# Feed-forward stage of a routed-expert kernel: eight written-out experts become one loop per engine

## The chip, the cores and the metric

One core of one Trainium2 chip runs the whole program. The metric is the device time of one execution in microseconds (us); the time before is 436.52 us, the median of 3 runs (436.09 to 436.82).

## The reference, cut to what matters

```python
x = x + conv_attention(_ln_c(x))           # 2 x 256 channels x 1024 places
t = _to_tokens(x); xt = _ln_t(t)           # 2048 tokens of 256
gate = softmax(xt @ Wg)                    # 8 experts
topv, topi = top_k(gate, 2)                # two experts for each token
for e in range(8):
    h = gelu(xt @ W1[e] + b1[e])           # 256 -> 1024
    ye = h @ W2[e] + b2[e]                 # 1024 -> 256
    out = out + ye * scores[:, e:e + 1]    # zero but for the two chosen
x = _from_tokens(t + out, x)
```

The change touches the loop over experts and nothing ahead of it.

## The kernel before

The first part (layer norm, attention, gates) takes about 170 us. It ends by sorting tokens by expert: `row_in` and `row_out` hold, for each tile, the rows to gather and to add to, and `bounds` holds for each expert e where its tiles end and two flags. `odd` says that its first tile is wide (`WIDE` = 3 blocks of 128 rows, not 2), `more` that it has further tiles of two blocks. With this input there are 17 tiles t; experts 0, 1, 3 and 7 have three each, expert 5 two, experts 2, 4 and 6 one, and the first tile of experts 0 and 5 is wide.

The feed-forward stage has no barrier: five engines each run their own program over the same tiles and meet through semaphores. Each program is a Python loop over the eight experts that writes the code out eight times: for each expert a wide first tile (`If(odd)`), a narrow first tile (`Else`) and a loop over further tiles (`If(more)`, `Fori`). In one tile:

- PE (TensorE) does `tile` (L1546): four `layer1` groups, then by turns `layer2(j-4)` and `layer1(j)` up to j = 7, then `turn_x` of the next tile (L1511, six transposes), then the last four `layer2`. Each product is three matmuls of high and low parts (`product3`, L1237 to 1239; L1538 to 1542). `layer1` may run four groups ahead (`RING`); `layer2(j)` waits for `h_split` of its own j (L1530).
- ScalarE (ACT) does two GELUs for each j (L802, L805). In an expert's first tile it also takes the high part of the next expert's weights, one eighth (`PIECE`) for each j (L815). Bias is a column of `b1t`.
- VectorE (DVE) takes `h_lo` (L1187) and in first tiles the low part of the weights (L1194). When PE has ended the tile it adds b2 (`y_sum`, L1203), waits for GpSimd's `y_free` and multiplies by the score (`y_out`, L1211), and goes to the next tile's `h_lo`.
- GpSimd (POOL) waits for `turn_x`, gathers the rows of the tile after next (L533, three indirect DMAs), sets `idx_out` (L571), lets DVE go (`y_free`, L574) and adds `y_out` to the output with indirect DMAs (L579).
- SP loads the raw weights of expert e once the split of expert e-1 is done (`load_expert`, L346).

So DVE's instructions stand in this order at the seam of two tiles, and PE's first `layer2` of the new tile waits for the last:

```python
    for i in range(width):
        ins = dve.tensor_scalar(y_out[:, i, :], ...)      # waits y_free
# ... end of the tile, branches ...
    dve.wait_ge(gelu_done, t * HJ + (j + 1 + RING))
    dve.tensor_tensor(h_lo[:, j, 0:w], ...).then_inc(h_split, 1)
```

`expert_bounds` (L340) loads the word of an expert from SBUF into a register (`value_load`, a TENSOR_LOAD) and takes it apart. ACT and DVE load all eight words ahead of the stage (L823, L1174); PE and POOL load one at each expert (L1573, L584 and L586).

## Time and profile before

| | |
|---|---|
| median of 3 runs | 436.52 us (436.09 to 436.82) |
| the profiled execution, its own time | 437.19 us |
| its span in the profile | 435.4 us |
| busy: PE / weight load / DVE / ACT / POOL | 373.3 / 334.5 / 267.0 / 248.1 / 185.5 us |
| instruction fetches: PE's queue (q8) / the other engines' (q14) | 28 packets, 0.46 MB / 27 packets, 0.22 MB |

The sum of a prediction is made against 437.19 us, of which 1.8 us lie outside the span; that execution stands 0.67 us above the median. A time at the head of a row is us from the span's start. "Idle" in brackets is the time in which that engine did nothing ahead of the row, and the arrow names what ended it; "issue" means that nothing in the profile did. A name with q (DVEq, PEldq) is the sequencer of that engine: the small instructions that set registers, load a word or branch, which the page doesn't count as busy.

### The profile page before, as it was taken

Reading aid. Unit: us, or ns where it says so; the run is one execution under the profiler, and the core shown is the slowest. Engines: PE = TensorE matmul, PEld = TensorE weight load, DVE = VectorE, ACT = ScalarE, POOL = GpSimd, SP = SyncE. Lnnn points to the kernel's source line nnn. Section 1 sums busy time; section 2 is a strip of 40 time slices with the busy share of each in tenths; the row PEclk is TensorE's granted clock in tenths of the full one; section 3 lists DMA queues with packets and bytes.
Section 4 is the critical chain, followed back from the end, with each engine's and each line's share of the span. In section 5 each row is a group of like instructions: output and inputs, shape, how many; then the busy total and the mean of one; then the engine's idle time right before and its main releaser. Section 6 shows DMA issues by size and latency. Waiting matters only on the chain.

```text
span 435.4 us, 8097 instructions
## 1 busy us (share of the span) xinstructions
PE 373.3 (86%) x2476; PEld 334.5 (77%) x2476; DVE 267.0 (61%) x684; ACT 248.1 (57%) x522; POOL 185.5 (43%) x279
## 2 busy tenths in 40 slices
PE   5889969989998657899999999799997999899960
PEld 4435557877787646899989998799987998799960
DVE  4668478796898995275447447584365754734430
ACT  1386557647516752385567467486575846655530
POOL 4610000003056565316656557535565265636553
PEclk9699999999996555799999999899999999989995
DMA  8710000000020754708324733648326434322332
GB/s 273 226 36 2 0 1 2 0 2 1 2 96 2 293 169 139 250 6 254 63 53 78 205 58 62 184 98 237 63 52 178 92 54 64 53 41 52 49 53 32
DMA packets 22983, 38.91 MB, mean 89 GB/s; under 512 B 2576, under 2 KB 17296, under 8 KB 22800
## 3 DMA queue, kind: packets, MB, share of 16 engines
q1 hardware_dynamic: 14896, 25.41, 17.3%
q0 software_dynamic: 8032, 12.82, 17.1%
q8 instruction: 28, 0.46, 0.4%
q14 instruction: 27, 0.22, 0.2%
HBM read 28.85 MB, written 9.37 MB: 88 GB/s over the span
## 4 chain that ended last, share of the span: by engine, by line
PE 35%; issue 8%; POOL 8%; DMA 4%; DVE 1%; POOLq 1%; DVEq 1%; ACT 0%; ACTq 0%
POOL xg L533 7%; PE banks L1538 6%; PE banks L1237 6%; PE banks L1238 5%; PE banks L1239 5%; PE banks L1540 5%; PE banks L1542 5%; PE banks L1515 3%; DMA xg<-xn_rows,idx_in 3%; DMA out_rows<-y_out,idx_out 1%; DVE h_lo L1187 1%; PE banks L1571 1%; DVE y_out L1211 1%; POOL out_rows L579 0%; POOL idx_out L571 0%
## 5 line engine op out<-in xcount | busy, mean ns | idle before, releaser
L802 ACT ACTIVATE h_raw<-banks,b1t 128x256 f32<-128x256 f32 (+1 forms) x136 | 67.2, 494 | 88.0 <-PE banks L1239 87.3
L1187 DVE TENSOR_TENSOR h_lo<-h_raw,h_hi 128x256 fp32r<-128x256 f32 (+1 forms) x136 | 58.8, 443 | 68.0 <-ACT h_hi L805 67.0
L1538 PE MATMUL banks<-w_hi,h_hi 128*128 128x256 f32 x288 | 83.8, 291 | 5.7 <-DVE h_lo L1187 5.6
L1237 PE MATMUL banks<-x_hi,w_hi 128*128 128x256 f32 (+1 forms) x272 | 81.0, 298 | 8.3 <-issue 8.3
L1540 PE MATMUL banks<-w_lo,h_hi 128*128 128x256 f32 x288 | 81.3, 282 | 0.0
L1542 PE MATMUL banks<-w_hi,h_lo 128*128 128x256 f32 x288 | 81.3, 282 | 0.0
L1238 PE MATMUL banks<-x_lo,w_hi 128*128 128x256 f32 (+1 forms) x272 | 79.9, 294 | 0.9 <-issue 0.9
L1239 PE MATMUL banks<-x_hi,w_lo 128*128 128x256 f32 (+1 forms) x272 | 79.9, 294 | 0.0
L579 POOL DMA_INDIRECT out_rows<-y_out,idx_out x36 | 61.4, 1705 | 33.7 <-DVE y_out L1211 27.9
L533 POOL DMA_INDIRECT xg<-xn_rows,idx_in x57 | 56.4, 990 | 28.0 <-POOL idx_in L528 15.4
L805 ACT ACTIVATE h_hi<-banks,b1t 128x256 fp32r<-128x256 f32 (+1 forms) x136 | 66.9, 492 | 0.0
L1538 PEld LDWEIGHTS banks<-w_hi,h_hi 128*128 128x128 f32 x288 | 54.9, 191 | 8.0 <-DVE h_lo L1187 8.0
L1237 PEld LDWEIGHTS banks<-x_hi,w_hi 128*128 128x128 f32 x272 | 53.5, 197 | 9.4 <-issue 9.3
L1540 PEld LDWEIGHTS banks<-w_lo,h_hi 128*128 128x128 f32 x288 | 55.0, 191 | 0.0
L1542 PEld LDWEIGHTS banks<-w_hi,h_lo 128*128 128x128 f32 x288 | 54.9, 191 | 0.0
L1239 PEld LDWEIGHTS banks<-x_hi,w_lo 128*128 128x128 f32 x272 | 53.4, 196 | 1.0 <-issue 1.0
L1238 PEld LDWEIGHTS banks<-x_lo,w_hi 128*128 128x128 f32 x272 | 53.6, 197 | 0.0
L470 POOL TENSOR_TENSOR rt<-rstd_i,rhv 128x4 f32<-128x4 f32 x12 | 2.5, 211 | 97.9 <-DVE rstd_i L1002 97.3
L1194 DVE TENSOR_TENSOR w_lo<-w_raw,w_hi 128x512 fp32r<-128x512 f32 x56 | 38.6, 689 | 0.7
L815 ACT ACTIVATE w_hi<-w_raw 128x512 fp32r<-128x512 f32 x56 | 36.4, 650 | 0.0
L692 ACT ACTIVATE pt_hi<-banks 128x512 fp32r<-128x512 f32 x32 | 17.5, 596 | 20.9 <-PE banks L1352 20.9
L1179 DVE TENSOR_TENSOR x_lo<-banks,x_hi 128x768 fp32r<-128x768 f32 x18 | 17.2, 958 | 13.1 <-ACT x_hi L792 12.8
(217 smaller groups left out, 686.4 us busy)
## 6 DMA issues: line engine op xcount, KB each, us to landing
w_raw<-in_w SPq DMA_DIRECT2D x16, 1024.0 KB, 7.8
xn_rows<-xn SPq DMA_DIRECT2D x2, 1056.0 KB, 4.7
x<-in_x_tok SPq DMA_DIRECT2D x4, 512.0 KB, 5.8
out_rows<-x SPq DMA_DIRECT2D x1, 2048.0 KB, 9.3
b2b<-in_b SPq DMA_DIRECT2D x1, 1024.0 KB, 4.4
xg<-xn_rows,idx_in POOLq DMA_INDIRECT x57
out_rows<-y_out,idx_out POOLq DMA_INDIRECT x36, 3.9
out_rows<-x POOLq DMA_DIRECT2D x1, 384.0 KB, 3.2
```

The lines of the kernel that those rows point to most:

```text
L533: pool.indirect_dma_start(xg[:, i, :], None, xs_d, bass.IndirectOffsetOnAxis(ap=idx_in[:, i:i + 1], axis=0)).then_inc(x_gathered, 16)
L579: pool.indirect_dma_start(out_d, bass.IndirectOffsetOnAxis(ap=idx_out[:, i:i + 1], axis=0), y_out[:, i, :], None, compute_op=ALU.add).then ...
L802: act.activation(h_raw[j % RING][:, 0:w], banks[:, j % RING, 0:w], ACT.Gelu, bias=bias)
L805: act.activation(h_hi[:, j, 0:w], banks[:, j % RING, 0:w], ACT.Gelu, bias=bias).then_inc(gelu_done, 1)
L1187: dve.tensor_tensor(h_lo[:, j, 0:w], h_raw[j % RING][:, 0:w], h_hi[:, j, 0:w].bitcast(F32), ALU.subtract).then_inc(h_split, 1)
L1194: dve.tensor_tensor(w_lo[(e + 1) % 2][:, c], w_raw[(e + 1) % 2][:, c], w_hi[(e + 1) % 2][:, c].bitcast(F32), ALU.subtract).then_inc(w_spli ...
L1237: pe.matmul(out, a_hi, b_hi, start=start, stop=False)
L1238: pe.matmul(out, a_hi, b_lo, start=False, stop=False)
L1239: return pe.matmul(out, a_lo, b_hi, start=False, stop=stop)
L1538: pe.matmul(out, h_hi[:, j, r], w_hi[e % 2][:, c], start=j == 0 and i < 2, stop=False, skip_group_check=width == WIDE)
L1540: pe.matmul(out, h_hi[:, j, r], w_lo[e % 2][:, c], start=False, stop=False, skip_group_check=width == WIDE)
L1542: ins = pe.matmul(out, h_lo[:, j, r], w_hi[e % 2][:, c], start=False, stop=j == HJ - 1, skip_group_check=width == WIDE)
```

## The change

PE runs a loop of four rounds over pairs of experts, with the two experts of a pair written out; ACT, DVE and POOL run a loop of eight rounds over one expert. What hung on a Python number now hangs on a register:

- each engine loads the expert's word of `bounds` inside the loop; the word now also holds the first tile;
- the two weight buffers become one tile with an index, fixed on PE (`odd` is 0 or 1 in the pair), chosen by a register on ACT and DVE; `w_loaded` is one semaphore that only grows, and SP waits for one load before it issues the next;
- ACT copies the expert's eight bias columns to `b1e` ahead of each expert and waits for that copy;
- DVE picks b2's and the score's columns by register;
- the last expert, too, splits "the next" weights (nobody reads that result), so one branch of the code is gone.

```diff
         def expert_bounds(eng, e):
-            word = eng.value_load(bounds[0:1, 0, e:e + 1], min_val=4, max_val=4 * TMAX + 3)
-            return word // 4, word % 4 // 2, word % 2
+            word = eng.value_load(bounds[0:1, 0, bass.ds(e, 1)], min_val=4, max_val=132 * TMAX + 3)
+            first = nc.s_assert_within(word // 128, 0, TMAX - 1, skip_runtime_bounds_check_because=why)
+            after = nc.s_assert_within(word % 128 // 4, 1, TMAX, skip_runtime_bounds_check_because=why)
+            return first, after, word % 4 // 2, word % 2
...
         def _(sp):
...
+                sp.wait_ge(w_loaded, 32 * e)
                 load_expert(sp, e)
+            sp.wait_ge(w_split, HJ * (E - 1))
+            sp.wait_ge(w_loaded, 32 * E)
+            sp.sem_inc(w_loaded, 32)
...
         def _(pool):
...
-            for e in range(E):
-                t1, odd, more = expert_bounds(pool, e)
-                odd1 = pool.value_load(bounds[0:1, 1, e:e + 1], min_val=0, max_val=E)
+            with pool.Fori(0, E) as e:
+                t0, t1, odd, more = expert_bounds(pool, e)
+                wides = pool.value_load(bounds[0:1, 1, bass.ds(e, 1)], min_val=0, max_val=17 * E)
+                odd0, odd1 = wides // 16, wides % 16
...
         def _(act):
...
-                    bias = b1t[:, e * HJ + j:e * HJ + j + 1]
+                    bias = b1e[:, j:j + 1]
...
-                    if split and e + 1 < E:
+                    if split:
                         if j == 0:
-                            act.wait_ge(w_loaded[(e + 1) % 2], 32 * ((e + 1) // 2 + 1))
+                            act.wait_ge(w_loaded, e * 32 + 64)
                             act.wait_ge(l2_done, t * HJ + HJ)
+                            act.sem_inc(splits_begun, 1)
...
-                        act.activation(w_hi[(e + 1) % 2][:, c], w_raw[(e + 1) % 2][:, c], ACT.Copy
-                                       ).then_inc(whi_done, 1)
+                        to = bass.ds((e + 1) % 2, 1)
+                        act.activation(w_hi[:, to, c].rearrange("p a c -> p (a c)"),
+                                       w_raw[:, to, c].rearrange("p a c -> p (a c)"), ACT.Copy).then_inc(whi_done, 1)
...
-            experts = [expert_bounds(act, e) for e in range(E)]
...
-            for e in range(E):
-                t1, odd, more = experts[e]
+            with nc.Fori(0, E, engines=[act.engine], head_slot={act.engine: 0}) as e:
+                t0, t1, odd, more = expert_bounds(act, e)
+                act.wait_ge(gelu_done, t0 * HJ + RING)
+                act.sem_inc(splits_begun, 1)
+                act.activation(b1e[:, :], b1t[:, bass.ds(e * HJ, HJ)], ACT.Copy).then_inc(b1_ready, 1)
+                act.wait_ge(b1_ready, e + 1)
...
         def _(dve):
...
-                    if split and e + 1 < E:
+                    if split:
...
-                        dve.wait_ge(whi_done, HJ * (e + 1) + j + 1)
+                        dve.wait_ge(whi_done, HJ * e + (HJ + j + 1))
...
-                                            b2b[:, e * C:(e + 1) * C], ALU.add)
+                                            b2b[:, bass.ds(e * C, C)], ALU.add)
...
-                    ins = dve.tensor_scalar(y_out[:, i, :], y_sum[:, i, :], score[:, i, e:e + 1], None, ALU.mult)
+                    ins = dve.tensor_scalar(y_out[:, i, :], y_sum[:, i, :], score[:, i, bass.ds(e, 1)], None, ALU.mult)
...
-            for e in range(E):
-                t1, odd, more = experts[e]
+            with nc.Fori(0, E, engines=[dve.engine], head_slot={dve.engine: 0}) as e:
+                t0, t1, odd, more = expert_bounds(dve, e)
...
         def _(pe):
...
-            for e in range(E):
-                t1, odd, more = expert_bounds(pe, e)
-                with pe.If(odd):
-                    tile(t0, e, WIDE, True)
...
+            with pe.Fori(0, E // 2) as pair:
+                for n in range(2):
+                    e = pair * 2 + n
+                    t0, t1, odd, more = expert_bounds(pe, e)
+                    with pe.If(odd):
+                        tile(t0, e, n, WIDE, True)
...
```

The static program of PE shrinks from 3,239 rows (runs of equal instructions) to 1,063, DVE's from 1,063 to 417, ACT's from 938 to 251 and POOL's from 497 to 163.

DVE, the seam between an expert's last tile and the next expert's first. An ISA row is a register operation. Before:

```order
L1211 TENSOR_SCALAR y_out<-y_sum,score 128x256 [waits y_taken,scores_moved,y_free]
L1211 TENSOR_SCALAR y_out<-y_sum,score 128x256
L1228 ISA
L1228 COMPARE_AND_BRANCH
L1227 UNCONDITIONAL_BRANCH
L1223 ISA
L1223 COMPARE_AND_BRANCH
L1185 ISA
L1186 REGISTER_ALU [waits gelu_done]
L1187 TENSOR_TENSOR h_lo<-h_raw,h_hi 128x384 [waits l2_done]
```

And now, the end of the round and behind it the head of the next (to which the branch of L1235 goes back):

```order
L1226 REGISTER_ALU [waits y_taken,scores_moved,y_free]
L1226 TENSOR_SCALAR y_out<-y_sum,score 128x256
L1226 ISA
L1226 TENSOR_SCALAR y_out<-y_sum,score 128x256
L1242 ISA
L1242 COMPARE_AND_BRANCH
L1241 UNCONDITIONAL_BRANCH
L1235 REGISTER_ALU
L1235 COMPARE_AND_BRANCH
```

```order
L1235 ISA
L344 TENSOR_LOAD bounds
L344 ISA x2
L1237 ISA
L1237 COMPARE_AND_BRANCH
L1197 ISA
L1198 REGISTER_ALU [waits gelu_done]
```

Between the wait for `y_free` and the first `h_lo` there now stand also a register operation ahead of each `y_out`, the count and branch of the outer loop, and the load of the expert's word, which stood ahead of the whole stage before.

ACT, the same seam, before (its load stood ahead of the stage) and now:

```order
L792 ACTIVATE x_hi<-banks 128x768 [waits xg_turned]
L829 ISA [waits bias_loaded]
L829 COMPARE_AND_BRANCH
L802 ACTIVATE h_raw<-banks,b1t 128x384 [waits h_split,l1_ready]
```

```order
L835 ISA
L344 TENSOR_LOAD bounds
L344 ISA x2
L837 ISA
L839 ISA [waits gelu_done]
L839 ACTIVATE b1e<-b1t 128x8
L840 REGISTER_ALU
L841 ISA [waits b1_ready]
L841 COMPARE_AND_BRANCH
```

ACT gains the load, the bias copy and a wait for its own copy, ahead of each expert's first GELU.

## Rows read from the trace of the kernel before

**Rows 1.** The page, busy time: engine, us, share of the span, instructions.
```profile
PE 373.3 (86%) x2476; PEld 334.5 (77%) x2476; DVE 267.0 (61%) x684; ACT 248.1 (57%) x522; POOL 185.5 (43%) x279
```

**Rows 2.** Waits, 180 to 436 us: engine and line, releaser: us, times, longest.
```profile
PE banks L1237 <- issue: 8.3, 5, 2.5
...
PE banks L1538 <- DVE h_lo L1187: 5.6, 10, 1.0
```

**Rows 3.** Timeline of PE, `turn_x` of nine tiles: start us, us.
```profile
259.24 0.82 PE L1515 MATMUL banks<-ident,xg 128*128 128x128 f32 x6
272.69 0.82 PE L1515 MATMUL banks<-ident,xg 128*128 128x128 f32 x6
289.08 0.82 PE L1515 MATMUL banks<-ident,xg 128*128 128x128 f32 x6
...
314.78 0.49 PE L1515 MATMUL banks<-ident,xg 128*128 128x128 f32 x3
328.23 0.82 PE L1515 MATMUL banks<-ident,xg 128*128 128x128 f32 x6
347.01 0.82 PE L1515 MATMUL banks<-ident,xg 128*128 128x128 f32 x6
361.63 0.82 PE L1515 MATMUL banks<-ident,xg 128*128 128x128 f32 x6
375.26 0.82 PE L1515 MATMUL banks<-ident,xg 128*128 128x128 f32 x6
391.41 0.82 PE L1515 MATMUL banks<-ident,xg 128*128 128x128 f32 x6
```

**Rows 4.** Timeline of PE, matmuls behind a pause: the pause stands in brackets.
```profile
213.85 0.38 PE L1538 MATMUL banks<-w_hi,h_hi 128*128 128x256 f32 x1 [0.44 <-DVE h_lo L1187]
...
266.83 0.39 PE L1538 MATMUL banks<-w_hi,h_hi 128*128 128x256 f32 x1 [1.01 <-DVE h_lo L1187]
278.85 0.56 PE L1237 MATMUL banks<-x_hi,w_hi 128*128 128x256 f32 x1 [2.48 <-issue]
...
334.29 0.43 PE L1237 MATMUL banks<-x_hi,w_hi 128*128 128x384 f32 x1 [2.38 <-issue]
353.84 0.28 PE L1238 MATMUL banks<-x_lo,w_hi 128*128 128x256 f32 x1 [0.87 <-issue]
...
381.18 0.49 PE L1237 MATMUL banks<-x_hi,w_hi 128*128 128x256 f32 x1 [2.24 <-issue]
```

**Rows 5.** Timeline of DVE at the seam of experts 1 and 2.
```profile
265.20 0.62 DVE L1211 TENSOR_SCALAR y_out<-y_sum,score 128x256 f32<-128x256 f32 x2 [1.39 <-POOLq L574]
...
266.35 0.43 DVE L1187 TENSOR_TENSOR h_lo<-h_raw,h_hi 128x256 fp32r<-128x256 f32 x1 [0.54 <-ACT h_hi L805]
```

**Rows 6.** Sequencers, by line: count, ns min/median/max, first and last start us.
```profile
L1574 PEldq COMPARE_BRANCH  x10: 73/348/2818, 178.7 to 378.3; - x10
...
L343 DVEq TENSOR_LOAD <-bounds x8: 297/304/558, 170.0 to 174.6; - x8
...
L1223 DVEq COMPARE_BRANCH  x1: 72/72/72, 265.6 to 265.6; - x1
...
L1185 DVEq FUSED_REGOPS  x1: 106/106/106, 266.1 to 266.1; - x1
L1185 DVEq ALU_OP  x1: 40/40/40, 266.4 to 266.4; - x1
...
L1228 DVEq FUSED_REGOPS  x2: 63/79/95, 212.8 to 213.2; - x2
L1228 DVEq COMPARE_BRANCH  x1: 69/69/69, 213.0 to 213.0; - x1
```

**Rows 7.** Windows: us, length, busy (x) of five engines, granted clock, DMA share, GB/s.
```profile
279.00:282.00 3.00, 3.00 (x15) 3.00 (x16) 0.79 (x4) 1.49 (x4) 1.64 (x1) 0.50 0.93 346
...
332.00:335.00 3.00, 0.71 (x4) 0.72 (x5) 1.37 (x4) 0.00 (x0) 1.80 (x3) 1.00 0.94 272
...
382.00:385.00 3.00, 3.00 (x17) 3.00 (x17) 0.42 (x1) 1.68 (x4) 1.99 (x2) 0.55 0.25 41
```

More of the change, by code:

```diff
@@ L119, in metaformer_kernel @@
         s_w = ctx.enter_context(ExitStack())
-        w_hi = [sb(f"w_hi{i}", [P, WCOLS], F32R, s_w) for i in range(2)]
-        w_lo = [sb(f"w_lo{i}", [P, WCOLS], F32R, s_w) for i in range(2)]
+        w_hi = sb("w_hi", [P, 2, WCOLS], F32R, s_w)
+        w_lo = sb("w_lo", [P, 2, WCOLS], F32R, s_w)
         with ExitStack() as s:
@@ L226, in metaformer_kernel @@
         bias_loaded = sem("bias_loaded")
-        w_loaded = [sem(f"w_loaded{i}") for i in range(2)]
+        b1_ready = sem("b1_ready")
+        w_loaded = sem("w_loaded")
+        splits_begun = sem("splits_begun")
         consts_made = sem("consts_made")
@@ L593, in _ @@
                         tile(t, e, t * 2 + odd1, 2)
-                t0 = t1
-                odd0 = odd1
-            pool.wait_ge(y_added, t1 * 32 + odd1 * 16 + 16)
-            pool.wait_ge(x_gathered, (t1 + 2) * (16 * WIDE))
+            last = expert_bounds(pool, E - 1)[1]
+            wide = pool.value_load(bounds[0:1, 1, E - 1:E], min_val=0, max_val=17 * E) % 16
+            pool.wait_ge(y_added, last * 32 + wide * 16 + 16)
+            pool.wait_ge(x_gathered, (last + 2) * (16 * WIDE))
         @block.scalar
@@ L814, in tile @@
                             x_high(t + 1)
-                        act.activation(w_hi[(e + 1) % 2][:, c], w_raw[(e + 1) % 2][:, c], ACT.Copy
-                                       ).then_inc(whi_done, 1)
-                if not (split and e + 1 < E):
+                        to = bass.ds((e + 1) % 2, 1)
+                        act.activation(w_hi[:, to, c].rearrange("p a c -> p (a c)"),
+                                       w_raw[:, to, c].rearrange("p a c -> p (a c)"), ACT.Copy).then_inc(whi_done, 1)
+                if not split:
                     x_high(t + 1)
@@ L1173, in _ @@
             dve.wait_ge(bounds_ready, 2)
-            experts = [expert_bounds(dve, e) for e in range(E)]
             def x_low(n):
@@ L1517, in turn_x, with layer1 @@
                 ins.then_inc(xg_turned, 1)
-            def layer1(t, e, j, width):
+            def layer1(t, odd, j, width):
                 pe.wait_ge(gelu_done, t * HJ + (j + 1))
@@ L1537, in layer2, with tile @@
                     out = banks[:, 4 + i % 2, i // 2 * C:(i // 2 + 1) * C]
-                    pe.matmul(out, h_hi[:, j, r], w_hi[e % 2][:, c], start=j == 0 and i < 2, stop=False,
+                    pe.matmul(out, h_hi[:, j, r], w_hi[:, odd, c], start=j == 0 and i < 2, stop=False,
                               skip_group_check=width == WIDE)
-                    pe.matmul(out, h_hi[:, j, r], w_lo[e % 2][:, c], start=False, stop=False,
+                    pe.matmul(out, h_hi[:, j, r], w_lo[:, odd, c], start=False, stop=False,
                               skip_group_check=width == WIDE)
-                    ins = pe.matmul(out, h_lo[:, j, r], w_hi[e % 2][:, c], start=False, stop=j == HJ - 1,
+                    ins = pe.matmul(out, h_lo[:, j, r], w_hi[:, odd, c], start=False, stop=j == HJ - 1,
                                     skip_group_check=width == WIDE)
                 ins.then_inc(l2_done, 1)
-            def tile(t, e, width, new):
+            def tile(t, e, odd, width, new):
                 pe.wait_ge(x_split, t + 1)
@@ L1567, in _ @@
             pe.wait_ge(bounds_ready, 2)
-            t0 = 0
             turn_x(0)
```

63 lines of the change are left out of this document (32 added, 31 removed).

## Prediction

> **What bounds the kernel now.** I read the page first: PE is busy 86% of the span [rows 1], so time is gained only where PE stands still. The waits from 180 us on, the feed-forward stage, say where it does: 8.3 us in five pauses that nothing in the profile ends, and 5.6 us in ten waits of `layer2` for `h_lo` [rows 2]. The timeline of PE gives the places [rows 4]. Three long pauses, 2.48, 2.38 and 2.24 us, stand ahead of the first tiles of experts 3, 5 and 7, each right behind a single-tile expert (2, 4, 6), whose loop code is jumped over. One of 0.87 us is in expert 5's second tile. The reader is to see what these pauses are: a compare-and-branch on PE's sequencer, usually 348 ns, took up to 2818 ns [rows 6]. I take that for the wait for code: it happens where code is skipped, and never in a loop's second pass.
>
> The other pauses have another owner. At the seam of experts 1 and 2 I follow the order of the code: `turn_x` at 259.24 [rows 3], then POOL's gathers, then `y_out` at 265.20 (5.96 us behind the turn), then `h_lo` at 266.35 [rows 5], then PE's first `layer2` at 266.83 after 1.01 us of waiting [rows 4]. So from one turn to the first `layer2` it is 7.59 us, set by POOL and DVE and not by PE, which was there at 6.58. DVE's own part is 1.15 us from `y_out` to `h_lo`, and the multiply is only 0.62 of it: the rest is branches and registers. A tile inside a loop waits on the same chain, for 0.44 us [rows 4]. **Any instruction added between `y_out` and `h_lo` is paid in full, at every tile.**
>
> I measure from turn to turn [rows 3]. Seams with no code pause take 13.45 us (expert 2: 259.24 to 272.69; expert 4: 314.78 to 328.23); expert 1, whose rows aren't shown, I take as equal. Expert 3 takes 16.39, expert 7 16.15, expert 6 13.63, the wide tile of expert 5 18.78.
>
> **What goes.** With loops, code is fetched once and the long pauses go. But PE then runs into the DVE chain, which it missed before because it was late. A seam can't be shorter than the 13.45 us of an undisturbed one, so of the pauses of 2.48 and 2.24 us experts 3 and 7 give back 2.94 and 2.70 (part of it is the clock, below), expert 6 0.18. Expert 5 gives back at most its 2.38, its second tile at most 0.87.
>
> **What comes, on DVE, part by part.**
> - In every tile: a register operation (40 ns) takes over the wait for `y_free`, and a fused one (106 ns) stands between the `y_out`s [rows 6]. With some 50 ns between instructions I take 0.2 us.
> - At each seam, the outer loop's count and branch: 40 ns and 72 ns, and the landing. A taken branch in the inner loop lands within 0.13 us (213.07 to 213.2), one over the wide tile's code needs 0.43 (265.67 to 266.1) [rows 6]. From both sides: 0.3 to 0.6 us with the gaps. The way back to the head is longer than either, so I take a value near the upper one.
> - At each seam, a fused operation for the address: 0.15 us.
> - At each seam, the load of the word. One takes 304 ns, but what stands behind it has to be done too: eight groups of load, unpacking and assertion began between 170.0 and 174.6 us, 0.66 us apart [rows 6]. They cost nothing there, since DVE waited for the first gather; in the loop nothing covers them.
>
> Sum for a seam: 0.2 + 0.3 to 0.6 + 0.15 + 0.66 = 1.3 to 1.6; I take 1.5 us. The Trainium skill (Advanced Engine Details and Errata, Control Flow Timing) gives about 108 ns for a compare-and-branch; by it the seam would be 1.2 us and the total below some 2 us less. The trace shows 72 ns for the instruction and up to 0.5 us until the next one, and I go by the trace.
>
> **What comes elsewhere.** PE: one load group and, in every second seam, the way back of the pair loop, some 0.1 to 0.6 us later at the first `layer1`. It waits for `h_lo` 1.01 + 1.5 us later on, which covers this. ACT: load group, bias copy, a wait for it, some 2.5 us in all by DVE's prices; ACT is free from the end of its `x_hi` until the next tile's first group, about as long, and `h_lo` of j = 0 now comes 1.5 us later than it did, so a late GELU is covered. POOL has two loads as before. SP's new wait is for a load that ended tens of us before. The last expert's split costs ACT and DVE eight pieces each, as in every other expert, and PE nothing but what the other seams show. The first `bounds` load of DVE falls between `x_lo(0)` and the first GELU; nothing.
>
> **Sum.** Experts 1, 2 and 4: 3 x 1.5 = +4.5. Expert 6: 13.45 + 1.5 against 13.63 = +1.3. Expert 3: 14.95 against 16.39 = -1.4. Expert 7: 14.95 against 16.15 = -1.2. Expert 5: `layer1` of a wide tile is half as long again (24 matmuls of 384 columns, not 256, at 2.4 GHz: 1.3 us more), so PE is there at 6.6 + 1.3 = 7.9 and `h_lo` at 7.6 + 1.5 = 9.1: the pause of 2.38 becomes one of 1.2, -1.2. Its second tile: -0.8. The other eight loop tiles at 0.2, less one behind a wide tile that has room: +1.4. The last `y_out`: +0.2. Together **+2.8 us**, and this holds already: about 9 us of pauses go and about 12 come.
>
> **The clock.** After the pause of 2.48 us the granted clock was 0.50 from 279 to 282, after the one of 2.24 it was 0.55 from 382 to 385; after the one of 2.38 it stayed at 1.00 [rows 7]. So a pause of this size halves the clock (2.4 to 1.2 GHz) sometimes, for some 3 us, and costs half of that, 1.5 us. The six narrow seams will now have pauses of 2.0 to 2.5 us at the first `layer2`, where three stood before. Nothing covers the loss there. Between no fall and six (0 to +9 us) I take one or two, **+2.2 us**, near what two falls in three pauses say for the seams with the longest pauses.
>
> In all +5.0: the profiled execution would be at 442.2, and since it stands 0.67 us above the median, the forecast is **441.5 us**.
>
> **Rivals.**
> - *The seam is cheap, and the kernel faster.* If the branch back lands at once and the load runs beside the `y_out`s, a seam costs 0.9 instead of 1.5: 7 x 0.6 = 4.2 less, with no fall of the clock 1.4 below before, 435.1 us. It decides below about 1.1 us a seam. For it: the multiply's 0.62 us could cover something. Against it: in the row of before `h_lo` comes 0.53 us after the `y_out`s have ended, so the sequencer was already the later one, and every addition stands behind it. Chance 0.10.
> - *The clock doesn't fall.* Then 436.5 + 2.8 = 439.3. For it: the pause of 2.38 us left the clock alone, and PE's late start splits the pause in two. Chance 0.22. The reverse, a fall at nearly every seam: 436.5 + 2.8 + 9 = 448. Chance 0.07.
> - *The code isn't kept.* Each way back could fetch its code anew. DVE's seven at 2.2 to 2.5 us (the pauses of rows 4) are 15 to 17 more, 455 us or over. Against it: an inner loop's second pass never shows such a pause. But these loops are far shorter. Chance 0.06. The Trainium skill (Runtime: NRT & Kernel Launch, Instruction fetch mechanics) speaks for this rival: it tells of a window of two pages with no reuse, out of which a taken branch stalls. No run here shows yet what a long loop does. If only PE fetches again, the DVE chain hides most of it and the forecast stands.
> - *The change does nothing:* the pauses stay as they are and the additions are covered, within 0.9 us of before. Chance 0.05.
>
> **How the numbers follow.** The forecast (seams longer, one to three falls, 439.5 to 445) has 0.50. A measurement of this kernel can tell about 0.2%, 0.9 us, from no change. Faster takes the first rival, 0.10; the same 0.07, from the last one and the edge of the first; slower 0.83. The range leaves out the cheap seam below and the many falls and new fetches above: 437 to 446.5.
>
> **What would show it.** No pause over 1 us "<- issue" on PE behind single-tile experts; at each narrow seam `layer2` waiting 2.0 to 2.5 us for `h_lo`; from `y_out` to `h_lo` some 2.6 us instead of 1.15; TENSOR_LOAD rows of DVE spread over the stage, eight in number; turn to turn about 14.9 us at seams; a granted clock of 0.5 behind some. Instruction fetches of PE's queue far below 28. Wrong would be: waits for `h_lo` at seams near 1 us, or fetches at every round.

## The result, and the profile after

| | before | changed |
|---|---|---|
| median, runs | 436.67 us, 4 | 448.65 us, 4 (445.98 to 449.0) |
| ratio | 1 | 1.0261 (1.0219 to 1.0303) |
| profiled execution, its span | 437.19, 435.4 us | 448.8, 447.1 us |
| fetches, PE's queue / the others' | 28 / 27 packets | 11 / 12 packets |

Slower by 2.6%, 12 us. The sign was forecast; the size (441.5, range up to 446.5) was not. The spans differ by 11.7 us, and the question is where these lie.

The page of the changed kernel, busy time (against [rows 1]), fetch queues, and its waits from 180 us on (against [rows 2]):

```profile
PE 375.7 (84%) x2476; PEld 335.9 (75%) x2477; DVE 272.7 (61%) x694; ACT 255.2 (57%) x539; POOL 183.2 (41%) x280
...
q8 instruction: 11, 0.18, 0.2%
q14 instruction: 12, 0.10, 0.1%
```

```profile
PE banks L1551 <- DVE h_lo L1199: 11.8, 11, 2.8
...
ACT b1e L839 <- issue: 9.5, 8, 6.3
...
PE banks L1551 <- issue: 8.2, 5, 2.0
...
PE banks L1251 <- issue: 3.1, 1, 3.1
```

Two things to see. PE's waits for `h_lo` have doubled, from 5.6 to 11.8 us, and the 8.2 us that nothing ends stand at the same matmul, L1551, the first `layer2` of a tile. It is the same chain: at expert 2, `h_lo` ends at 277.14 us and PE starts at 277.20. And two single waits are new: ACT 6.3 us ahead of its first bias copy, PE 3.1 us ahead of a `layer1` matmul.

From turn to turn, as in [rows 3] (timeline of PE):

```profile
196.62 0.82 PE L1528 MATMUL banks<-ident,xg 128*128 128x128 f32 x6
211.55 0.82 PE L1528 MATMUL banks<-ident,xg 128*128 128x128 f32 x6
...
241.54 0.82 PE L1528 MATMUL banks<-ident,xg 128*128 128x128 f32 x6
...
268.52 0.82 PE L1528 MATMUL banks<-ident,xg 128*128 128x128 f32 x6
283.05 0.82 PE L1528 MATMUL banks<-ident,xg 128*128 128x128 f32 x6
299.10 0.82 PE L1528 MATMUL banks<-ident,xg 128*128 128x128 f32 x6
...
325.38 0.82 PE L1528 MATMUL banks<-ident,xg 128*128 128x128 f32 x6
339.94 0.82 PE L1528 MATMUL banks<-ident,xg 128*128 128x128 f32 x6
357.21 0.82 PE L1528 MATMUL banks<-ident,xg 128*128 128x128 f32 x6
371.89 0.82 PE L1528 MATMUL banks<-ident,xg 128*128 128x128 f32 x6
386.40 0.82 PE L1528 MATMUL banks<-ident,xg 128*128 128x128 f32 x6
402.43 0.82 PE L1528 MATMUL banks<-ident,xg 128*128 128x128 f32 x6
```

Subtracting neighbours, and the same for the other kernels of this study (us; "stage's first turn" runs from the first `turn_x` of all, at 176 to 179 us, to the one in expert 0's first tile):

| interval that ends with the turn of | before | changed | word_ahead | dve_written | pe_loop_only | pe_loop_slot | all_cures_200 |
|---|---|---|---|---|---|---|---|
| expert 0, first tile | 16.68 | 19.74 | 18.46 | 20.19 | 15.67 | 15.66 | 16.65 |
| expert 0, second tile | 13.60 | 14.93 | 14.94 | 13.74 | 13.66 | 13.72 | 14.50 |
| expert 1, first | 13.49 | 16.86 | 17.08 | 18.11 | 17.44 | 13.62 | 13.92 |
| expert 2 | 13.45 | 14.53 | 13.90 | 13.56 | 13.57 | 13.57 | 13.91 |
| expert 3, first | 16.39 | 16.05 | 14.18 | 13.61 | 13.85 | 13.85 | 14.27 |
| expert 3, third (a loop tile) | 12.80 | 13.12 | 13.15 | 12.96 | 12.88 | 12.88 | 13.25 |
| expert 4 | 13.45 | 14.56 | 13.89 | 13.53 | 13.54 | 13.55 | 13.91 |
| expert 5, first (wide) | 18.78 | 17.27 | 16.86 | 16.36 | 16.23 | 16.15 | 16.94 |
| expert 6 | 13.63 | 14.51 | 13.81 | 13.50 | 13.50 | 13.51 | 13.92 |
| expert 7, first | 16.15 | 16.03 | 13.89 | 13.67 | 13.80 | 13.79 | 15.76 |

The first interval also hangs on the clock. From 177 to 180 us it was granted 0.52 in before and 0.50 in the changed kernel, from 178.2 to 181.2 us 1.00 in pe_loop_only and pe_loop_slot; their first interval, 1.0 us below that of before, is probably shorter for this and not for the loop. The 20.19 and 18.11 us of dve_written each have a fall of the clock in them.

**Two thirds of the loss lie in the first round.** From the stage's first turn (176.57 and 176.88) to that of expert 1 (233.19 and 241.54) the changed kernel takes 8.0 us more. From there to the last turn, thirteen tiles, it takes 187.44 us against 184.22, 3.2 more. The other 0.4 lie outside.

*The entry.* Timeline of ACT, the start of the stage, and of PE behind it:

```profile
178.50 0.81 ACT L801 ACTIVATE x_hi<-banks 128x768 fp32r<-128x768 f32 x1 [7.92 <-PE banks L1528]
185.63 0.21 ACT L839 ACTIVATE b1e<-b1t 128x8 f32 x1 [6.32 <-issue]
186.24 0.58 ACT L811 ACTIVATE h_raw<-banks,b1e 128x384 f32<-128x384 f32 x1 [0.41 <-ACT b1e L839]
```

```profile
188.05 0.39 PE L1551 MATMUL banks<-w_hi,h_hi 128*128 128x256 f32 x1 [2.83 <-DVE h_lo L1199]
```

ACT's bias copy starts 6.32 us behind its last work, and nothing in the profile ends that time; packets of the fetch queue q14 begin at 182.8, 183.9 and 185.6 us inside it. PE stands 2.83 us. I had written that ACT's late GELU is covered.

*Expert 1.* One matmul of `layer1` runs, and then:

```profile
228.29 0.38 PE L1250 MATMUL banks<-x_hi,w_hi 128*128 128x256 f32 x1
231.79 0.37 PE L1251 MATMUL banks<-x_lo,w_hi 128*128 128x256 f32 x1 [3.12 <-issue]
231.96 0.41 PE L1252 MATMUL banks<-x_hi,w_lo 128*128 128x256 f32 x1
```

One packet of q8 begins at 229.4 and takes 1.0 us, inside the 3.12 us. The matmuls behind it take 0.41 us, not 0.28: the clock fell, as after the long pauses of before.

*A seam, to compare with [rows 5].* Timeline of DVE at the seam of experts 1 and 2:

```profile
274.58 0.62 DVE L1226 TENSOR_SCALAR y_out<-y_sum,score 128x256 f32<-128x256 f32 x2 [1.39 <-issue]
276.72 0.42 DVE L1199 TENSOR_TENSOR h_lo<-h_raw,h_hi 128x256 fp32r<-128x256 f32 x1 [1.52 <-ACT h_hi L814]
```

From `y_out` to `h_lo` it is 2.14 us, where it was 1.15; I had said 2.6. The seams of experts 2 and 4 grew by 1.08 and 1.11 us, where I had said 1.5. The sequencer's rows for the load, the way back and PE's way back (count, ns min/median/max):

```profile
L344 DVEq TENSOR_LOAD <-bounds x8: 302/313/568, 180.1 to 393.4; - x8
L344 DVEq FUSED_REGOPS  x8: 190/197/210, 180.7 to 393.7; - x8
```

```profile
L1235 DVEq COMPARE_BRANCH  x9: 56/59/72, 179.4 to 435.5; - x9
L1235 DVEq FUSED_REGOPS  x8: 63/63/69, 180.0 to 393.3; - x8
```

```profile
L1584 PEldq COMPARE_BRANCH  x4: 83/212/216, 270.5 to 431.0; - x4
```

From the end of the branch back at this seam (275.14) to the next instruction (275.36) it is 0.22 us, at the others 0.22 to 0.25, and no way back shows a pause of a microsecond: **the code of the loops stays.** The last packet of PE's fetch queue begins at 250.3 us, and the three rounds behind it run without one; the last of the other engines' queue begins at 208.4.

The clock, windows as in [rows 7]:

```profile
231.00:234.00 3.00, 2.21 (x11) 2.21 (x11) 0.34 (x2) 0.95 (x3) 1.63 (x1) 0.54 0.22 45
291.00:294.00 3.00, 2.24 (x14) 2.25 (x15) 2.72 (x6) 2.87 (x7) 2.69 (x3) 0.78 1.03 313
294.00:297.00 3.00, 3.00 (x19) 3.00 (x19) 2.23 (x5) 1.93 (x5) 1.01 (x3) 0.65 0.93 187
334.00:337.00 3.00, 2.92 (x24) 2.93 (x25) 3.00 (x8) 2.94 (x7) 2.67 (x3) 1.00 0.37 44
395.00:398.00 3.00, 2.90 (x13) 2.90 (x14) 3.00 (x8) 2.21 (x6) 2.69 (x3) 0.51 0.39 44
```

It fell at experts 1, 3 and 7, and stayed at experts 2, 4 and 6. So the seams of experts 3 and 7 still take 16 us, some 14.5 for the chain and 1.5 for the clock, though PE's code pause is gone there.

### The profile page after: what moved, and what is told of

It reads as the page before. It is cut to its first block, busy times and chain, and to the rows that moved or that the text cites. A ratio compares the mean times of both kernels' runs of the same rounds, so it can differ in the third digit from the quotient of the medians.

```text
span 447.1 us, 8582 instructions
## 1 busy us (share of the span) xinstructions
PE 375.7 (84%) x2476; PEld 335.9 (75%) x2477; DVE 272.7 (61%) x694; ACT 255.2 (57%) x539; POOL 183.2 (41%) x280
## 4 chain that ended last, share of the span: by engine, by line
PE 39%; issue 9%; POOL 4%; DMA 3%; DVE 3%; DVEq 1%; POOLq 1%; ACTq 0%; ACT 0%
PE banks L1551 7%; PE banks L1555 7%; PE banks L1553 6%; PE banks L1250 5%; PE banks L1251 5%; PE banks L1252 5%; POOL xg L543 4%; PE banks L1528 3%; DMA xg<-xn_rows,idx_in 3%; DVE h_lo L1199 1%; DVE y_sum L1218 1%; DVE y_out L1226 1%; DVEq L1242 0%; POOL idx_in L538 0%; POOL idx_out L580 0%
## 5 line engine op out<-in xcount | busy, mean ns | idle before, releaser
L811 ACT ACTIVATE h_raw<-banks,b1e 128x256 f32<-128x256 f32 (+1 forms) x136 | 66.9, 492 | 82.2 <-PE banks L1252 79.2
L1551 PE MATMUL banks<-w_hi,h_hi 128*128 128x256 f32 x288 | 85.1, 295 | 20.0 <-DVE h_lo L1199 11.8
L588 POOL DMA_INDIRECT out_rows<-y_out,idx_out x36 | 60.3, 1675 | 36.5 <-DVE y_out L1226 30.7
L1551 PEld LDWEIGHTS banks<-w_hi,h_hi 128*128 128x128 f32 x288 | 55.6, 193 | 23.5 <-DVE h_lo L1199 14.1
L814 ACT ACTIVATE h_hi<-banks,b1e 128x256 fp32r<-128x256 f32 (+1 forms) x136 | 66.6, 490 | 0.0
L1207 DVE TENSOR_TENSOR w_lo<-w_raw,w_hi x64 | 44.0, 687 | 3.8 <-ACT w_hi L825 2.7
L825 ACT ACTIVATE w_hi<-w_raw x64 | 41.4, 647 | 0.0
L538 POOL COPY idx_in<-row_in 128x3 uint32 (+1 forms) x19 | 3.9, 204 | 59.9 <-PE banks L1528 56.2
```

The costliest lines, as they stand in the source:

```text
L588: pool.indirect_dma_start(out_d, bass.IndirectOffsetOnAxis(ap=idx_out[:, i:i + 1], axis=0), y_out[:, i, :], None, compute_op=ALU.add).then ...
L811: act.activation(h_raw[j % RING][:, 0:w], banks[:, j % RING, 0:w], ACT.Gelu, bias=bias)
L814: act.activation(h_hi[:, j, 0:w], banks[:, j % RING, 0:w], ACT.Gelu, bias=bias).then_inc(gelu_done, 1)
L1207: dve.tensor_tensor(w_lo[:, to, c].rearrange("p a c -> p (a c)"), w_raw[:, to, c].rearrange("p a c -> p (a c)"), w_hi[:, to, c].rearrange( ...
L1551: pe.matmul(out, h_hi[:, j, r], w_hi[:, odd, c], start=j == 0 and i < 2, stop=False, skip_group_check=width == WIDE)
```

## The experiments

The theory after this reading has four parts: DVE's longer chain at each tile and seam (half of it the load); falls of the clock behind the pauses that it makes; a cold entry of ACT; and a pause in expert 1 from where PE's code happens to lie. The rival: a loop on PE costs as such. The kernels before, running beside them, had medians of 436.6 to 437.3 us, single runs from 431 to 442; where the ratio's interval is too wide to tell, the turn-to-turn intervals of the profiles do.

### 1. Only PE looped (pe_loop_only)

```diff
-            with nc.Fori(0, E, engines=[dve.engine], head_slot={dve.engine: 0}) as e:
-                t0, t1, odd, more = expert_bounds(dve, e)
+            for e in range(E):                     # likewise ACT and POOL
+                t0, t1, odd, more = experts[e]
```

> ACT, DVE and POOL are written out eight times again, PE alone keeps its loop over pairs. Theory 1 (three parts: DVE's longer chain at seams, cold code in the first round, pauses of the written-out PE given back): the chain is that of before (`y_out` to `h_lo` 1.15 us, seams 13.45), ACT's entry isn't cold, so the first tile takes 3 us less than in the changed kernel; the pauses at experts 3, 5 and 7 are gone (-2.94, -2.3, -2.70, and -0.18 at expert 6, together -8.1); PE's own first-round pause in expert 1 stays (+2 to +3). Sum -5 to -6 against before: ratio about 0.987, 431 us. Theory 2 (PE's loop is what costs, by its late start and by the pause in expert 1, and the other loops are free): the time stays near that of the changed kernel, ratio over 1.015.

Measured: 434.47 us, ratio 0.9952 (0.9922 to 0.9981). The direction is right, and theory 2 falls: PE's loop makes the kernel faster. Seams are 13.5 to 13.85, experts 3, 5 and 7 give back 2.54, 2.55 and 2.35 us. The median is 3.5 us above what I said. The profile accounts for 1 to 2 us of that: the first-round pause of 3.43 us, with the clock fallen behind it, makes expert 1 take 17.44 us instead of 13.49, +3.95 where I had 2 to 3. The rest stays open. Timeline of PE:

```profile
224.28 0.38 PE L1247 MATMUL banks<-x_hi,w_hi 128*128 128x256 f32 x1
228.09 0.28 PE L1248 MATMUL banks<-x_lo,w_hi 128*128 128x256 f32 x1 [3.43 <-issue]
```

### 2. All but PE looped (pe_written)

```diff
-            with pe.Fori(0, E // 2) as pair:
-                for n in range(2):
-                    e = pair * 2 + n
+            for e in range(E):
```

> The changed kernel with PE written out eight times. Theory 1: the pause of 3.12 us in expert 1 goes (-2.3 of the seam's 3.37), the pauses of 2.2 to 2.5 at experts 3, 5 and 7 come back but stand beside the longer chain (+0.34, +1.5, +0.1 against the changed kernel); ACT's cold entry and the longer chain stay. Near the changed kernel, ratio to before 1.024 to 1.028, with seams at experts 2, 4, 6 of 14.3 to 14.5 us. Theory 2 (PE's loop costs): ratio near 1.00.

Measured: 453.82 us, ratio 1.0419 (1.0364 to 1.0475), the slowest of all. Theory 2 falls here too. My own figure was 5 to 7 us too low, most of it by the clock: it fell behind the entry's pause (3.08 us, matmuls of 0.41 and 0.52 us until 195, some 3 us lost) and at expert 4, behind a pause of 2.05 (16.06 us instead of 14.56). PE's pauses at experts 2, 3, 6 and 7 are 2.04, 2.16, 2.46 and 2.68 us. Its code pauses stand mostly beside the longer chain, not on top of it: experts 2 and 3 take 14.54 and 16.06 us, as in the changed kernel, experts 6 and 7 0.4 and 0.5 more.

### 3. No aligned loop heads on ACT and DVE (no_head_slot)

`head_slot` lays the first instruction of a loop at a given place of a block of code and jumps over what lies between.

```diff
-            with nc.Fori(0, E, engines=[act.engine], head_slot={act.engine: 0}) as e:
+            with nc.Fori(0, E, engines=[act.engine]) as e:        # likewise DVE
```

> The changed kernel without the alignment of the loop heads on ACT and DVE. If the first tile's 3 us come from the jump over the filling to the aligned head: the first `h_lo` 2.8 to 3 us earlier, ratio 1.019 to 1.021, 445.5 us. If any entry into code not run before costs this: no change, ratio 1.026. If the alignment is what keeps the code at hand on the way back: fetches of the other engines' queue at every round (over 20 packets instead of 12), pauses of ACT or DVE at seams, ratio over 1.03.

Measured: 446.66 us, ratio 1.0229 (1.0174 to 1.0284). Timeline of ACT at the entry:

```profile
179.84 0.81 ACT L801 ACTIVATE x_hi<-banks 128x768 fp32r<-128x768 f32 x1 [7.96 <-PE banks L1528]
181.10 0.21 ACT L839 ACTIVATE b1e<-b1t 128x8 f32 x1 [0.45 <-issue]
```

0.45 us instead of 6.32, and the first interval is 16.43 us instead of 19.74: the cold entry is the jump to the aligned head, worth 3.3 us. The other engines' queue had 10 packets, so the alignment isn't what keeps the code. The median fell by 2 us only: the profile has one more fall of the clock, at expert 6 (16.11 instead of 14.51).

### 4. Price of the load alone (before_load)

```diff
                 t1, odd, more = experts[e]
+                expert_bounds(dve, e)          # the kernel before; result unused
```

> The kernel before with one load of the expert's word and its unpacking, unused, on DVE at each seam; nothing is left out. If nothing hides the load (my theory): `y_out` to `h_lo` 1.15 + 0.66 = 1.8 us, the seams into experts 1, 2, 4 and 6 longer by 0.66 (expert 6 by 0.5), those into 3, 5 and 7 as before, since PE's pause is the later there: +2.5 us, ratio 1.0057. If the load runs beside the multiply (rival): under 0.3 us a seam, ratio under 1.003.

Measured: 437.22 us, ratio 1.0023 (0.9989 to 1.0056). That is a miss for the time: it lies in the rival's range, and my 1.0057 just outside the interval. The seams in the profile still bear out the theory. Timeline of DVE at the seam of experts 1 and 2:

```profile
267.62 0.62 DVE L1211 TENSOR_SCALAR y_out<-y_sum,score 128x256 f32<-128x256 f32 x2 [1.39 <-issue]
269.40 0.42 DVE L1187 TENSOR_TENSOR h_lo<-h_raw,h_hi 128x256 fp32r<-128x256 f32 x1 [1.16 <-issue]
```

1.78 us from `y_out` to `h_lo`, 0.63 more than in [rows 5]. The seams into experts 1, 2, 4 and 6 took 14.14, 14.06, 14.07 and 14.26, each 0.61 to 0.65 longer; experts 3, 5 and 7 were 0.3 to 0.4 shorter than before, their pauses being a little shorter in this run, and expert 5's second tile 0.96 shorter (13.66 instead of 14.62), without the pause that it had before. These took back what the load cost. The load is paid in full where no other pause stands above it.

### 5. Only PE looped, its head elsewhere (pe_loop_slot)

```diff
-            with pe.Fori(0, E // 2) as pair:
+            with nc.Fori(0, E // 2, engines=[pe.engine], head_slot={pe.engine: 100}) as pair:
```

> Only PE looped, as in pe_loop_only, and the head of its loop moved by some 80 instructions (head_slot 100). Why: in the changed kernel and in pe_loop_only the pause of expert 1 (3.12 and 3.43 us) stands behind the first matmul of its narrow tile, with one fetch inside it. Theory: the branch lands a few instructions ahead of the end of a piece of code that is there, and the next piece is asked for only on landing. Moved by 80, the landing lies deep inside a piece: the pause goes, and with it the fall of the clock behind it, expert 1's interval is 13.5 us instead of 17.4, the time 3.9 us below pe_loop_only: 430.6 us, ratio to before 0.986. Rival (any first pass through a piece of PE's code that a branch skips to costs this): the pause stays or appears elsewhere, ratio 0.995.

Measured: 431.33 us, ratio 0.9911 (0.9873 to 0.9949), **faster than both kernels**. Expert 1 takes 13.62 us. Timeline of PE, the longest pause there, and the waits of PE in the stage:

```profile
228.53 0.39 PE L1548 MATMUL banks<-w_hi,h_hi 128*128 128x256 f32 x1 [0.95 <-DVE h_lo L1196]
```

```profile
PE banks L1548 <- DVE h_lo L1196: 9.8, 14, 1.3
PE banks L1247 <- issue: 0.6, 3, 0.2
```

What stands still now is nearly all DVE's chain: 9.8 us in 14 waits, none over 1.3, and no fall of the clock up to the last turn.

### 6. A placement meant to be bad (pe_loop_slot10)

The same edit with 10 in place of 100.

> Only PE looped, its loop head this time 9 instructions ahead of where it lies in pe_loop_only. There one matmul of expert 1's narrow tile ran, and the pause of 3.43 us stood ahead of the second. Theory (the end of a piece of code lies right behind the landing): with a matmul and its weight load being two instructions, four to five more of the tile run first and the pause stands ahead of the fifth to seventh matmul; it stays 2.5 to 3.4 us, with slow matmuls behind it, the interval of expert 1 at 16.7 to 17.4, ratio 0.994 to 0.997, 434 us. Rival (any moving of the head cured it in pe_loop_slot, by chance): no pause, or one elsewhere, ratio 0.991.

Measured: 441.55 us, ratio 1.0131 (1.0048 to 1.0214). Timeline of PE, expert 1's first matmuls:

```profile
232.55 0.38 PE L1247 MATMUL banks<-x_hi,w_hi 128*128 128x256 f32 x1
232.76 0.28 PE L1248 MATMUL banks<-x_lo,w_hi 128*128 128x256 f32 x1
...
233.24 0.28 PE L1249 MATMUL banks<-x_hi,w_lo 128*128 128x256 f32 x1
235.65 0.28 PE L1247 MATMUL banks<-x_hi,w_hi 128*128 128x256 f32 x1 [2.13 <-issue]
```

Six matmuls ran (three are left out here), then the pause, where one had run before: with the head some nine instructions nearer to the start of its block (by the estimate below), the pause came five matmuls later. The place is as forecast. The length (2.13) and the price weren't (expert 1 takes 14.66 us, with no fall of the clock), and a cost that I hadn't thought of came in:

```profile
187.40 0.68 PE L1247 MATMUL banks<-x_hi,w_hi 128*128 128x384 f32 x1 [5.81 <-issue]
```

PE's own entry is now cold. As I read it, the head no longer lies in the block in which the code ahead ends, as with 100, but in the next, and PE stands 5.81 us at the jump to it, much as ACT stood 6.32. The first interval is 22.59 us instead of 15.66. Not all of the 6.9 us are the jump: the clock was granted 0.50 from 184 to 190 us, so that the first 3 us of PE's work behind the pause ran at half speed (some 1.5 us, an estimate).

The Trainium skill (Runtime: NRT & Kernel Launch, Instruction fetch mechanics) gives blocks of 256 instructions, 16 KiB, for these fetches, and PE's queue agrees: 0.18 MB in 11 packets. In PE's program, with a matmul counted as two, expert 1's narrow tile begins some 1,000 instructions behind the head. By blocks of that size it would begin at 1,010 for a head at 10, fourteen short of the fourth boundary, and at 1,019 for the head of pe_loop_only, if that is at 19, five short. This is an estimate, and the 19 is a guess. The trace agrees with it roughly: the pauses of experiments 1 and 6 stand behind one and behind six matmuls.

### 7. All loops, PE's head moved, no other alignment (all_loops_slot)

> The changed kernel with PE's loop head moved as in pe_loop_slot and without the alignment on ACT and DVE. Theory (first round costs two separate things, ACT's entry by the alignment and PE's landing in expert 1): 11.7 - 3.3 - 3.9 = 4.5 us above before, ratio 1.010, 441.4 us; seams as in the changed kernel (14.5 us at experts 2 and 4). Rival (the pauses come from loops as such): ratio 1.022 to 1.026.

Measured: 444.54 us, ratio 1.0194 (1.0119 to 1.0269), between the two. Both cures worked (first interval 17.23 us; no code pause in expert 1), but the clock fell at four seams, experts 1, 3, 6 and 7, behind pauses of 1.97, 2.10, 1.74 and 2.47 us, all at the first `layer2`: 16.12, 16.18, 16.10 and 16.47 us instead of 14.6. With expert 1's code pause gone, the chain's own pause stood in its place. This profile is of the slowest of five executions, 448.58 us; the other four took 442.44 to 444.7, so the clock probably fell less often in them.

### 8. DVE loads the word ahead (word_ahead)

```diff
+            word_reg = dve.alloc_register("next_word")
...
+                        if j == 5:        # in an expert's first tile
+                            dve.reg_mov(word_reg, dve.value_load(bounds[0:1, 0, bass.ds(e + 1, 1)], ...))
...
-                t0, t1, odd, more = expert_bounds(dve, e)
+                t0, t1, odd, more = split_word(dve.snap(word_reg, ...))
```

> The changed kernel, but DVE loads the next expert's word during the first tile, ahead of its seventh `h_lo`, and carries it in a register; the seam has no load. If the load is 0.66 us of the seam's growth (as it was in before_load): `y_out` to `h_lo` 1.5 us instead of 2.14, each of seven seams 0.6 to 0.66 shorter, 4.4 us in all, ratio 1.016, 444.2 us. If something else comes last at the seams once DVE is earlier (ACT's load, bias copy and wait): less than 0.3 a seam and PE's waits at seams ended by ACT, ratio 1.022 or more.

Measured: 442.34 us, ratio 1.0149 (1.0072 to 1.0226). Timeline of DVE, seam of experts 2 and 3, and the window behind it:

```profile
288.73 0.62 DVE L1236 TENSOR_SCALAR y_out<-y_sum,score 128x256 f32<-128x256 f32 x2 [1.54 <-POOLq L589]
290.19 0.46 DVE L1206 TENSOR_TENSOR h_lo<-h_raw,h_hi 128x256 fp32r<-128x256 f32 x1 [0.84 <-ACT h_hi L820]
```

```profile
291.00:294.00 3.00, 3.00 (x27) 3.00 (x27) 3.00 (x7) 3.00 (x8) 2.69 (x3) 1.00 1.06 337
```

1.46 us instead of 2.14, seams of 13.90, 13.89 and 13.81 at experts 2, 4 and 6, 0.63 to 0.7 less each. Experts 3 and 7 gave back 1.87 and 2.14, as their pauses sank to 1.65 and 1.33 and the clock stayed at 1.00. So, in these two profiles, **0.66 us of DVE's sequencer was worth 2.0 us where the clock fell with it and not without it.**

### 9. DVE alone written out (dve_written)

> The changed kernel with DVE alone written out eight times; ACT, POOL and PE keep their loops, the last expert has no low split. Theory 1 (DVE's chain owns the seams and the loop tiles): `y_out` to `h_lo` 1.15 to 1.2 us, seams of experts 2, 4 and 6 at 13.5, loop tiles 12.85 to 12.9; ACT's cold entry (3 us) and PE's pause in expert 1 (3.9) stay; 11.7 - 6 = 5.5 above before, ratio 1.012 to 1.014, 442.5 us. Theory 2 (ACT's additions at the seam matter as much): seams stay over 14.2, ratio over 1.02. The first tile tells whether DVE's or ACT's entry is the cold one: unchanged 3 us if ACT's.

Measured: 437.14 us, ratio 1.0022 (0.9985 to 1.006), 5 us below what I expected. Theory 1 has the direction right and gave too small a gain. The profiled execution was the slowest of ten, 440.75 us, with the clock fallen in the first tile and for longer in expert 1. In it, seams take 13.5 to 13.67 us and third tiles 12.9, and with the shorter pauses (0.63 to 0.83 us at experts 2, 3, 4, 6 and 7) no fall of the clock at experts 3 and 7. ACT's loop, with its load, bias copy and wait at each seam, costs nothing there: PE's waits at seams are no longer than those of pe_loop_only. The entry is ACT's, since DVE has no loop here:

```profile
186.59 0.21 ACT L839 ACTIVATE b1e<-b1t 128x8 f32 x1 [5.90 <-issue]
```

### 10. No register operation at the multiply (fixed_column)

```diff
-                    ins = dve.tensor_scalar(y_out[:, i, :], y_sum[:, i, :], score[:, i, bass.ds(e, 1)], None, ALU.mult)
+                    ins = dve.tensor_scalar(y_out[:, i, :], y_sum[:, i, :], score[:, i, 0:1], None, ALU.mult)
```

> The changed kernel, but `y_out` multiplies with column 0 of the scores for every expert, so that DVE needs no register operation ahead of its multiplies (the output carries the wrong scores). Theory (these operations stand in every tile's chain): loop tiles 12.87 us instead of 13.14, seams 0.2 to 0.3 shorter, 16 tiles together 4 us; where a seam's pause sinks from 2.0 below 1.8, the clock's fall may go too, 1.5 each at experts 3 and 7: 442 to 444.5 us, ratio 1.012 to 1.018. Rival (the loop tiles' 0.28 comes from elsewhere, such as the branch back or PE): loop tiles stay at 13.13, ratio 1.022 or more.

Measured: 444.28 us, ratio 1.0141 (1.0088 to 1.0195). The third tiles of experts 0, 1, 3 and 7 take 12.90 to 12.97 us instead of 13.12 to 13.18, the seams of experts 2 and 4 14.31 and 14.33 instead of 14.53 and 14.56. That is 0.2 per tile, 3.5 us in seventeen tiles; the medians differ by 4.4. The 0.28 by which a loop tile had grown is explained for the most part, not in full. The clock fell at expert 7 (pause of 1.89) and not at expert 3 (1.96).

### 11 and 12. All loops with all cures (all_cures, all_cures_200)

PE's head at 100 and at 200, no other alignment, the word loaded ahead.

> All loops kept, with three cures: PE's loop head moved (as pe_loop_slot), no alignment on ACT and DVE, DVE's word loaded ahead (as word_ahead). Theory (the loss of the changed kernel is entry 3.3, expert 1's pause and clock 3.2 to 3.9, the load 0.63 at each seam, and 1.5 for each fall of the clock behind a pause of 2 us): from word_ahead's 442.3 the first two go, seams of experts 1, 2, 4, 6 and 7 at 13.9, none with slow matmuls behind it, 435.5 us, ratio to before 0.995 to 1.001. Rival (the clock falls at seams whatever their length, as at experts 1, 3, 6 and 7 of all_loops_slot): four intervals of 15.5 us, ratio 1.010 or more.

> As all_cures, but PE's loop head another 100 instructions later. In the profile of all_cures expert 1 still had a pause of 2.64 us, ahead of its first matmul, with PE's fetch inside it, which pe_loop_slot, at the same place of the head, had 16 us earlier. Theory: there the piece is asked for only in the last 3 us or so of an inner round, and the branch back can come first; at this place of the head it is asked for in the first third of the inner loop, and expert 1 has no pause ended by nothing: its interval 13.9 to 14.1 us instead of 15.06. The seam of expert 3 keeps 14.2 if the clock doesn't fall, 15.7 if it does. 437 to 438 us, ratio 0.997 to 1.001. Rival (the fetch comes late by chance wherever the head lies): the pause stays, ratio 1.002.

Measured: 438.58 us, ratio 1.0022 (0.9992 to 1.0052), and 437.79 us, 1.0041 (1.0010 to 1.0072). The first is 3 us above the 435.5 that I expected. The second's time is as expected, its ratio (0.997 to 1.001 expected) higher, since the runs of before beside it were faster (436.59). The two agree within their intervals, so the times don't show what moving the head to 200 is worth; the profiles show what it did in expert 1. In the profile of the first, expert 1 had a pause of 2.64 us ahead of its first matmul, with a packet of PE's queue at 226.0 inside it; in the second it is gone:

```profile
230.63 0.39 PE L1563 MATMUL banks<-w_hi,h_hi 128*128 128x256 f32 x1 [1.26 <-DVE h_lo L1206]
```

and expert 1 takes 13.92 us instead of 15.06, as expected. That the early request was lost to the branch back, in the first, is argued from two profiles, not shown. In each of them one seam still met a fall of the clock (expert 3, pause of 1.73; expert 7, of 1.79).

### Pauses and clock over all profiles

The first 20 us of the stage are left out here, since in most profiles the clock was already low as the stage began. Counted in the fourteen profiles, from 200 us on, are PE's pauses of 1 us and more, and whether matmuls behind them took 0.40 us and over instead of 0.28 (12 to 23 of them):

| pause, us | count | with the clock fallen behind |
|---|---|---|
| 1.00 to 1.69 | 38 | 0 |
| 1.73 to 1.89 | 12 | 6 |
| 1.96 to 2.19 | 12 | 8 |
| 2.24 to 3.43 | 14 | 11 |

The length alone doesn't decide: at the seam of expert 3 a pause of 1.73 us was followed by a fall in all_cures and not in all_cures_200. The two intervals, 15.75 and 14.27 us, also tell what such a fall costs: 1.5.

## Why the prediction was right in its sign and wrong in its size

**Right: the chain, and what it does to the long pauses.** From expert 1's turn on, my terms were, without the clock: experts 2 and 4 +3.0, expert 6 +1.3, experts 3, 7 and 5 -1.4, -1.2 and -2.0, six loop tiles +1.2, together +0.9; with the 2.2 for the clock +3.1. Measured are +3.2 ([rows 3] against the rows above). That the sums agree so closely is luck, since the errors of the parts cancel. The seams of experts 2, 4 and 6 grew by 3.1 together, not 4.3. Six loop tiles grew by 2.1, not 1.2, and expert 5's second tile gave back nothing, where I had 0.8. Experts 3 and 7 gave back 0.3 and 0.1: the clock fell there, where it had fallen before as well, which took the place of the 2.2 that I had for new falls.

**The terms of a seam.** The load: 0.66 forecast, 0.61 to 0.65 by before_load, 0.63 to 0.7 by word_ahead. The register operations in the `y_out` part: 0.2 forecast, 0.2 by fixed_column. What is left of 1.08 for the branch back and the address is 0.2 to 0.25, where I had 0.3 to 0.6 and 0.15: mis-sized. I took a value near the upper end because the way back is long; it took 0.22 us from the end of the branch to the next instruction, less than the 0.43 of a shorter jump before. And I missed a gain. At the seam of experts 1 and 2 the count, the way back and the address took 0.46 us together, but the jump over the wide tile's code, 0.43 us from branch to next instruction in [rows 6] (265.67 to 266.1), now takes 0.13 (276.37 to 276.5). The sequencer's rows:

```profile
L1237 DVEq COMPARE_BRANCH  x1: 66/66/66, 276.3 to 276.3; - x1
...
L1197 DVEq FUSED_REGOPS  x1: 98/98/98, 276.5 to 276.5; - x1
```

It is so at nearly every narrow seam: 0.45 to 0.50 us in before (0.14 at expert 7), and from expert 2 on in pe_loop_only and dve_written, where DVE is written out too; 0.14 in the changed kernel and 0.20 in no_head_slot. Why is not shown.

**Right: the code is kept.** 28 packets became 11 on PE's queue and 27 became 12 on the others', none of PE's behind 250.3 us. The Trainium skill's rule for this rival (Runtime: NRT & Kernel Launch, Instruction fetch mechanics: two pages, no reuse, a stall for a taken branch out of the window) doesn't hold for PE's loop here, of some 1,450 instructions (counted in its program): three rounds ran without a fetch. The same section gives PE room for 2,048 instructions, into which such a loop would fit, and the trace agrees with that. It also agrees that a branch to code which isn't there stalls: 6.32 us at ACT's entry with the jump, 0.45 without.

**Wrong: the first round of the loops.** Three steps failed, each by pricing a loop's steady round and never its first one: that ACT's "late GELU is covered", which holds at a seam and not at the entry; that expert 1 would pay the seam's 1.5 like experts 2 and 4; and that the tile behind the wide one "has room" and costs nothing. My sum had 1.5 + 0.2 us for the whole stretch up to expert 1's turn; 8.0 were measured. These 6.3 are nearly all of the 6.6 us by which the profiled execution (448.8) lies above my figure for it (442.2).

Where code is first reached by a jump it has to be fetched once, and the changed kernel jumps to an aligned head on ACT (3.3 us, by no_head_slot) and, on PE, over the wide tile of its second expert to a place where only one matmul runs before the next fetch (3.8 us with the clock, 17.44 against 13.62, by pe_loop_slot). The pauses of [rows 4] had told me what such a fetch costs, 2.2 to 2.5 us; I used that only as a gain.

Of the 8.0, 3.1 fall in the first tile, 3.4 in expert 1 (with a fall of the clock in it), 1.3 in the tile behind the wide one and 0.3 in the third. The 1.3 are more than the chain's 0.2 to 0.3 for a loop tile. That tile takes 14.09 to 14.94 us in every kernel with DVE's loop and 13.60 to 13.81 in those with DVE written out, but for pe_loop_slot10 (14.43, 0.56 of it a code pause of PE's own). So it goes with DVE's loop, but which of its instructions make it stays open: no run took them apart there.

**The clock: a right term with the wrong handle.** I had none to six falls, with one or two as the likely number, over narrow seams with pauses of 2.0 to 2.5 us. Pauses were shorter, 1.65 to 2.03, and three falls came: one new, at expert 1, behind a code pause, and two that had been there before. What I lacked is in the table above: the pauses that the change made have the lengths behind which the clock sometimes fell and sometimes didn't, and so the same edit costs 0.63 or 2.0 us.

**Rivals.** The cheap seam is nearest to what seams did (1.08, and it was to decide below 1.1), but the kernel wasn't faster, because of the first round. The rival with a fall at nearly every seam forecast 448, and that the time came out there is chance: two of the six narrow seams had a fall behind a wait for `h_lo`. The late start of PE was covered, as said (a start 0.2 us later at experts 2, 4 and 6, and intervals of 13.57 and 13.54 in pe_loop_only against 13.45). ACT's additions in a steady round cost nothing, as said (dve_written).

## What to carry to other kernels

Price a loop's first round apart from its steady one: where does each engine enter it, over what does it jump, and does that lie in code that is already there? A head that had to be jumped to in a block not yet there cost 3.3 us on ACT and 6.9 on PE (some 1.5 of it by the clock, an estimate), once; one moved within reach cost nothing and removed a pause of 3.4 us. And look at how long the pauses are that an edit leaves, not only at their sum: 0.66 us less at a seam was worth 2 us where the clock no longer fell. Loop only the engine whose code fetches stand on the critical path: here PE's loop alone is worth 1% (431.33 us), while DVE's loop, on the chain between multiply and `h_lo`, costs some 2.5% (448.65 us with it, 437.14 without).

## What the runs showed of the hardware that was not expected

- Entering a loop through a jump into a block not yet fetched: 6.32 us on ACT, 5.81 us on PE, 5.90 us on ACT again with DVE written out, against 0.45 us without the jump. That is over twice the 2.2 to 2.5 us of a skipped tile in [rows 4].
- The place of a fetch pause follows the place of the code: a loop head some nine instructions nearer to the start of its block (an estimate, experiment 6) moved it from behind the first matmul to behind the sixth.
- A jump of DVE's over the wide tile's code took 0.45 to 0.50 us at five of six narrow seams of before, 0.14 at all of the changed kernel.
- From 200 us on, of 38 pauses of PE between 1.00 and 1.69 us none was followed by a fall of the clock, of 26 from 1.96 us up 19 were; a fall costs about 1.5 us at a seam (15.75 against 14.27, behind the same pause of 1.73).
